# One block of gated attention and a mixture of experts on one core: the shared expert of a block runs behind the MLP of the next, weight splits move to VectorE, two normalizations share one chain, and q stays unnormalized

## The reference

```python
x = x + ln(attn(ln(x)))              # x: 2048 tokens x 256, ln: no weight, eps 1e-5
x = x + ln(moe(ln(x)))

def attn(x):                         # 16 heads of 16
    h = ln(x) * ln1w + ln1b
    xc = silu(causal_conv(h, 4 taps))
    q, k = l2norm(h @ Wq), l2norm(h @ Wk)          # per head, eps 1e-12
    v = ln_head(h @ Wv) * vnw + vnb
    u = sigmoid(xc @ Wig + big) * k * v
    mem = scan(m_t = gamma_t * m_(t-1) + u_t)      # gamma = sigmoid(xc @ Wg + bg)
    out = (ln_head(mem) * mnw + mnb) * q
    out = (ln_head(out) * gnw + gnb) * sigmoid(xc @ Wog + bog)
    h = x + out @ Wo
    return h + (silu(h2 @ Wgate) * (h2 @ Wval)) @ Wout     # h2 = ln(h)*ln2w+ln2b, width 1024

def moe(x):                          # 8 experts of width 176, the best 2; shared expert of width 704
    routed = sum of the 2 chosen experts, weighed by their softmax probabilities
    return routed + sigmoid(x @ shared_gate) * ((silu(x @ sg) * (x @ su)) @ sd)
```

## Time and profile before

| what | value |
|---|---|
| median of 3 runs | 705.24 us |
| the profiled execution: its own time | 704.88 us |
| its span, from the first to the last instruction | 703.1 us |
| PE busy | 557.0 us, 79% of the span |
| DVE busy | 417.2 us, 59% |
| ACT busy | 242.5 us, 34% |
| POOL busy | 128.3 us, 18% |
| chain that ended last | PE 50%, DVE 27%, issue 11%, POOL 6%, ACT 4% |

### The profile page before, as it was taken

The page is one execution under the profiler, slowest core; times in us unless marked ns, Lnnn a source line. Parts: engine busy times, 40 slices in busy tenths (PEclk is TensorE's granted clock), DMA queues, the critical chain, the costliest instruction groups (busy, mean ns, idle before and its releaser), DMA issues.

```text
span 703.1 us, 7640 instructions
## 1 busy us (share of the span) xinstructions
PE 557.0 (79%) x2332; PEld 417.0 (59%) x2332; DVE 417.2 (59%) x1313; ACT 242.5 (34%) x418; POOL 128.3 (18%) x120
## 2 busy tenths in 40 slices
PE   1742247995998998669999949999558999999493
PEld 1322035783876767458767827878446777777382
DVE  6386775348797467977637774711435455555147
ACT  3421335312537461226552224331012144444213
POOL 1142600112022012000513000210000423333300
PEclk9975667999799999959999976999858999999888
DMA  8940000000101000110100000010070233333343
GB/s 290 401 113 30 0 2 0 1 0 31 60 16 46 31 0 1 40 51 0 62 30 1 1 30 0 31 61 0 1 239 0 92 99 107 107 108 98 117 168 119
DMA packets 30570, 45.43 MB, mean 65 GB/s; under 512 B 3211, under 2 KB 25227, under 8 KB 30187
## 3 DMA queue, kind: packets, MB, share of 16 engines
q1 hardware_dynamic: 25539, 33.99, 14.9%
q0 software_dynamic: 3408, 9.38, 3.7%
q10 hardware_dynamic: 1584, 1.57, 0.7%
HBM read 28.60 MB, written 16.34 MB: 64 GB/s over the span
## 4 chain that ended last, share of the span: by engine, by line
PE 50%; DVE 27%; issue 11%; POOL 6%; ACT 4%; DMA 1%; POOLq 0%; DVEq 0%; ACTq 0%; SPq 0%
PE psum L682 11%; PE psum L647 8%; PE psum L648 7%; PE psum L649 7%; PE psum L707 6%; POOL y_routed L465 5%; PE psum L657 3%; DVE est L931 2%; PE psum L756 2%; DVE IG L1157 2%; PE psum L742 2%; PE psum L728 1%; DVE rt L912 1%; DVE rt L911 1%; PE psum L882 1%
## 5 line engine op out<-in xcount | busy, mean ns | idle before, releaser
L1215 DVE TENSOR_TENSOR SM<-SM,psum 128x512 f32<-128x512 f32 (+1 forms) x56 | 38.1, 683 | 85.5 <-ACT SM L576 85.3
L576 ACT ACTIVATE SM<-psum 128x512 f32<-128x512 f32 (+1 forms) x56 | 33.1, 595 | 147.2 <-PE psum L649 117.9
L456 POOL DMA_INDIRECT x_dispatched<-XN,dest x32 | 33.1, 1033 | 260.3 <-DVE XN L1278 251.8
L682 PE MATMUL psum<-WOU,SM 128*128 128x256 f32 x256 | 59.8, 379 | 0.0
L707 PE MATMUL psum<-WQKV,HT 128*128 128x512 f32 (+1 forms) x128 | 50.7, 544 | 8.1 <-ACT GA L563 3.3
L682 PEld LDWEIGHTS psum<-WOU,SM 128*128 128x128 f32 x256 | 48.2, 189 | 8.4 <-DVE SM L1215 0.5
L833 PE MATMUL psum<-RUP,GX 128*128 x156 | 52.7, 460 | 0.4 <-DVE GX L1293 0.4
L465 POOL DMA_INDIRECT y_routed<-GO,g_dest x39 | 37.9, 971 | 69.0 <-ACT GO L624 68.4
L682 PE MATMUL psum<-SDN,SM 128*128 128x256 f32 (+1 forms) x192 | 45.0, 381 | 0.7 <-DVE SM L1215 0.7
L647 PE MATMUL psum<-XTH,supH 128*128 128x512 f32 (+1 forms) x96 | 44.2, 460 | 0.8 <-issue 0.8
L707 PEld LDWEIGHTS psum<-WQKV,HT 128*128 128x128 f32 x128 | 26.3, 211 | 30.4 <-issue 24.3
(11 more groups left out here) (257 smaller groups left out, 1223.0 us busy)
## 6 DMA issues: line engine op xcount, KB each, us to landing
XG<-x_dispatched SPq DMA_DIRECT2D x39, 130.0 KB
YF<-y_routed SPq DMA_DIRECT2D x4, 1024.0 KB, 9.1
RUP<-rup SPq DMA_DIRECT2D x1, 2816.0 KB
X<-x SPq DMA_DIRECT2D x4, 512.0 KB, 6.8
x_after_attention<-X SPq DMA_DIRECT2D x4, 512.0 KB, 3.4
XF<-x_after_attention SPq DMA_DIRECT2D x1, 2048.0 KB, 8.1
out<-XF SPq DMA_DIRECT2D x4, 512.0 KB, 2.9
QKV<-x ACTq DMA_DIRECT2D x3, 512.0 KB, 3.6
```

The source lines that it names most:

```text
L456: nc.gpsimd.indirect_dma_start(XD[:, :], bass.IndirectOffsetOnAxis(dest[:, i, old + j:old + j + 1], 0), XN[:, j, :], None).then_inc(dispat ...
L682: last = nc.tensor.matmul(p_down[:, j // 2, (j % 2) * D:(j % 2 + 1) * D], SM[0:rows, g % 3, j * P:(j + 1) * P], weight[0:rows, m, :], star ...
L1215: nc.vector.tensor_tensor(SM[0:rows, g % 3, 0:tb], SM[0:rows, g % 3, 0:tb], p_pair(n)[1][0:rows, 0:tb], ALU.mult).then_inc(hid_ready, 1)
```

## The change

1. **The order.** The list of steps is now one list `ORDER` for all blocks. The shared expert of block b-1 stands behind `x2` of block b, ahead of `xt` of block b; `choose` and `rank` of b-1 stand among the MLP products of block b. In block 0 nothing stands behind `x2`. The shared expert of the last block comes last, as before. Since two steps now mix blocks, the counters (`HIDX`, `SLOT`, `done`) come from the list. `PLACE` has new numbers for it.
2. **Weight splits.** The `lo` halves are computed on DVE: two of the three weights after the first two tiles of `q` in block 0, the third (`sup`) among block 0's MLP products. In block 0, PE writes the four tiles of `q` into four different pairs of banks and no longer waits for ACT's copies.
3. **LayerNorms.** `ln0` computes both reciprocal roots in one chain of 8 values per token row. With v the variance, the root of the second LayerNorm is taken from (1 + eps) * v + eps * eps.
4. **q.** q is not divided by its norm. GpSimd multiplies each tile of q by the weight and by the bias of the norm as soon as ACT has squared it (three multiplications for a tile, with that of v; before: one, and three large ones later). The norm enters as the eps of the last LayerNorm per head, `qeps`, and `rs` treats 128 values instead of 192.
5. **Last pass.** `FIN` is two groups of 8 tiles.

```diff
+def _order():
+    def shared(b, at_rank):
+        out = []
+        for i in range(SMN + 3):
+            out += [("hid", b, i)] if i < SMN else []
+            out += [("sdn", b, i - 3)] if i >= 3 else []
+            out += [("rank", b, 0), ("choose", b, 3)] if i == 2 and at_rank else []
+        return out + [("shout", b, 0)]
+    order = []
+    for b in range(NB):
+        late = {0: [("choose", b - 1, 1)], 1: [("choose", b - 1, 2)], 2: [("rank", b - 1, 0), ("choose", b - 1, 3)]} if b > 0 else {}
+        for m in range(FM):
+            order += [("mup", b, m)] + ([("mdn", b, m - 1)] if m > 0 else []) + late.get(m, [])
+            order += [("split", 0, 2)] if (b, m) == (0, 4) else []
+        order += [("mdn", b, FM - 1), ("sum", b, 0), ("sum", b, 1), ("x2", b, 0), ("x2", b, 1)]
+        if b > 0:
+            order += shared(b - 1, False)
+        order += [("xt", b, 0), ("route", b, 0), ("choose", b, 0)]
...
-        [0, 2, 3, 4, 8, 13, 16, 16, 16, 16, 16, 17, 20, 21, 21, 21, 25, 25, 25, 26, 27, 27, 28, 30, 30, 33, 33,
+        [0, 0, 2, 2, 2, 2, 2, 2, 3, 3, 3, 3, 3, 4, 4, 4, 5, 6, 8, 8, 8, 8, 11, 11, 11, 11, 12,
...
-FIN = (4, 4, 4, 4)
+FIN = (8, 8)
...
# GpSimd, step q (scan on GpSimd is gone)
-                    nc.gpsimd.tensor_tensor(vj, vj, hvec[:, 0, :].unsqueeze(1).broadcast_to([P, HEADS, HD]),
-                                            ALU.mult).then_inc(v_scaled, 1)
-                        link(nc.gpsimd.tensor_tensor(q, q, per_head(rr[:, 0:nj, 0:HEADS]), ALU.mult))
-                        nc.gpsimd.tensor_tensor(k, q, per_dim(nj, 2), ALU.mult).then_inc(g_ready, 1)
-                        nc.gpsimd.tensor_tensor(w, q, per_dim(nj, 3), ALU.mult).then_inc(g_ready, 1)
+                    link(nc.gpsimd.tensor_tensor(heads(QB[:, m:m + 1, :]), qj, per_dim(1, 3), ALU.mult))
+                    nc.gpsimd.tensor_tensor(qj, qj, per_dim(1, 2), ALU.mult).then_inc(q_scaled, 1)
+                    nc.gpsimd.tensor_tensor(vj, vj, per_dim(1, 0), ALU.mult).then_inc(v_scaled, 1)
...
# VectorE
+                if stage == "split" and b == 0:
+                    k, _ = resident[m]
+                    dve.wait_ge(w_hi, m + 1)
+                    for c in range(C):
+                        nc.vector.tensor_tensor(lo[k][:, c, :], raw[k][:, c, :], f32(hi[k][:, c, :]), ALU.subtract).then_inc(w_lo, 1)
...
+                        step(rsqrt(r01[:, b % 2, :, 0:nj], *own))
...
+                        step(nc.vector.scalar_tensor_tensor(va[:, 0:G], va[:, 0:G], 1.0 / HD, qeps[:, 0:G], ALU.mult, ALU.add))
...
                 if stage == "wo":
+                    if b > 0:
+                        dve.wait_ge(x2_ready, b)
                     nc.vector.tensor_tensor(flat(HR[:, 0:nj, :]), flat(p_main)[:, 0:nj * D], flat(HN[:, 0:nj, :]), ALU.add).then_inc(hr_ready, 1)
...
# TensorE
                 if stage == "xt":
+                    if b > 0:
+                        pe.wait_ge(sh_ready, old)
```

More of the change, by code:

```diff
@@ L56 @@
 ATTENTION = (
-    [("q", j) for j in range(J)] + [("rs", 0), ("rs", 1), ("g", 0), ("g", 1)]
-    + [("u", i) for i in range(4)] + [("ut", 0), ("scan", 0), ("scan", 1), ("mt", 0), ("split", 0)]
-    + [("var", 0), ("rstd", 0), ("norm", 0), ("fetch", 0), ("g", 2), ("affine", 0), ("affine", 1), ("split", 1), ("split", 2)]
+    [("q", 0), ("split", 0), ("q", 1), ("split", 1)] + [("q", j) for j in range(2, J)] + [("rs", 0), ("rs", 1), ("g", 0), ("g", 1)]
+    + [("u", i) for i in range(4)] + [("ut", 0), ("scan", 0), ("scan", 1), ("mt", 0)]
+    + [("var", 0), ("rstd", 0), ("norm", 0), ("fetch", 0), ("g", 2), ("affine", 0), ("affine", 1)]
     + [("mean", 1), ("centre", 1), ("ln0", 0), ("var", 1), ("rstd", 1), ("norm", 1), ("og", 0), ("y0", 0), ("ln0", 1)]
@@ L63 @@
 AHEAD = [("ln0", i) for i in range(3)] + [("fetch", 0), ("ht", 0), ("xs", 0)] + [("conv", k) for k in range(KC)]
[L66 to L75, removed]
+def _order():
[16 more added lines that the diff above has]
+        order += [("xt", b, 0), ("route", b, 0), ("choose", b, 0)]
+    last = shared(NB - 1, True)
+    return order + last[:1] + [("choose", NB - 1, 1)] + last[1:3] + [("choose", NB - 1, 2)] + last[3:]
+ORDER = _order()
+HIDX = {step: g for g, step in enumerate(s for s in ORDER if s[0] in ("mup", "hid"))}
+SLOT = {step: n for n, step in enumerate(s for s in ORDER if s[0] in ("mup", "hid", "rank"))}
 PLACE = {
@@ L124, in steps @@
                  for i, s in enumerate(ATTENTION) if 0 <= b + (s in AHEAD) < NB]
-    experts = [(name, b, m) for b in range(NB) for name, m in EXPERTS[TILES[b]]]
-    for n, step in enumerate(experts):
+    for n, step in enumerate(ORDER):
         while attention and attention[0][0] <= n:
@@ L187, in build @@
         hst, hmv = sb("hst", [P, J, 6]), sb("hmv", [P, J, 2])
-        hva, hrs, hrt = (sb(k, [P, J]) for k in ("hva", "hrs", "hrt"))
+        hva, hrs, hrt = (sb(k, [P, 2, J]) for k in ("hva", "hrs", "hrt"))
         vec = sb("vec", [P, C, NVEC])
@@ L292, in v, with done @@
             return vec[:, c, i:i + 1]
-        def slot(b, h):
-            return SLOTS * b + h + (h >= FM + RANK_AT)
-        def rank_slot(b):
-            return SLOTS * b + FM + RANK_AT
         resident = [("wgt", 16), ("wvl", 16), ("sup", 16)]
-        W_UP, W_SHARED = 2, 3
+        W_UP, W_SHARED = 2 * C, 3 * C
         def hidden(stage, b, m):
-            h, rows = (m, P) if stage == "mup" else (FM + m, SM_ROWS[m])
-            return HIDDEN * b + h, slot(b, h), rows
+            step = (stage, b, m)
+            return HIDX[step], SLOT[step], P if stage == "mup" else SM_ROWS[m]
+        def done(stage, b, m):
+            return HIDX[(stage, b, m)] + 1
         block = ctx.enter_context(nc.Block())
@@ L361, in _ @@
                     load_x(b + 2)
-                if b + 1 < NB:
-                    sp.wait_ge(sh_ready, START[b + 1])
-                    sp.dma_start(tiles(SS, b), SH[:, 0:TILES[b], :]).then_inc(sh_kept, 16)
-            sp.wait_ge(up_psum, HIDDEN * (NB - 1) + FM)
+                if b > 0:
+                    sp.wait_ge(sh_ready, START[b])
+                    sp.dma_start(tiles(SS, b - 1), SH[:, 0:TILES[b - 1], :]).then_inc(sh_kept, 16)
+            sp.wait_ge(up_psum, done("mup", NB - 1, FM - 1))
             sp.wait_ge(x2_kept, 16 * NB)
@@ L430, in at @@
                     pool.wait_ge(sq_ready, old + m + 1)
[L431 to L450 removed]
+                    if b > 0 and m == 0:
+                        pool.wait_ge(wo_psum, b)
+                    qj, vj = heads(QKV[:, m:m + 1, 0:D]), heads(QKV[:, m:m + 1, 2 * D:3 * D])
+                    link(nc.gpsimd.tensor_tensor(heads(QB[:, m:m + 1, :]), qj, per_dim(1, 3), ALU.mult))
+                    nc.gpsimd.tensor_tensor(qj, qj, per_dim(1, 2), ALU.mult).then_inc(q_scaled, 1)
+                    nc.gpsimd.tensor_tensor(vj, vj, per_dim(1, 0), ALU.mult).then_inc(v_scaled, 1)
+                if (stage, m) == ("choose", 3):
                     pool.wait_ge(xn_ready, new)
@@ L519, in at @@
                         act.wait_ge(ss_done, n - 1)
+                    if b > 0 and m < 2:
+                        act.wait_ge(h2_lo, C * b)
                     nc.scalar.activation(SQ[n % 2], QKV[:, m, :], ACT.Square).then_inc(sq_ready, 1)
@@ L567, in at @@
                     if b > 0:
-                        act.wait_ge(up_psum, HIDDEN * (b - 1) + FM)
+                        act.wait_ge(up_psum, done("mup", b - 1, FM - 1))
                     for c in range(C):
@@ L587, in at @@
                     act.wait_ge(xt_psum, b + 1)
+                    if b > 0:
+                        act.wait_ge(up_psum, done("hid", b - 1, SMN - 1))
                     for c in range(C):
@@ L595, in at @@
                 if stage == "shout":
-                    act.wait_ge(hid_used, HIDDEN * (b + 1))
+                    act.wait_ge(hid_used, done("hid", b, SMN - 1))
                     act.wait_ge(shared_gate, b + 1)
@@ L706, in at @@
                         for c in range(C):
-                            last = nc.tensor.matmul(p_main[:, part, 0:cols.stop - cols.start], HT[:, c, tok], WQKV[:, c, cols],
+                            last = nc.tensor.matmul(q_banks(b, m)[:, part, 0:cols.stop - cols.start], HT[:, c, tok], WQKV[:, c, cols],
                                                     start=c == 0, stop=c == C - 1)
@@ L795, in at @@
                 if stage == "rank":
-                    n = rank_slot(b)
+                    n = SLOT[("rank", b, 0)]
                     pair_free(n)
@@ L908, in newton @@
             def newton(a, y, t, out):
+                if len(out.shape) > len(a.shape):
+                    a, y, t = (ap.rearrange("p (j h) -> p j h", h=out.shape[2]) for ap in (a, y, t))
                 settle()
@@ L1115, in at @@
                     dve.wait_ge(sq_ready, n + 1)
-                    if b > 0 and m == 0:
-                        dve.wait_ge(g_ready, 2 * b)
                     nc.vector.tensor_reduce(rr[:, m, :], by_head(SQ[n % 2]), AX_X,
@@ L1260, in at @@
```

(4 more changed lines are left out.)

145 lines of the change are left out of this document (72 added, 73 removed), and 56 rows, old and new, of the table PLACE.

## The result

The changed kernel takes 680.56 us (median of 4 runs, 680.3 to 681.84), the kernel before 705.12 us: a ratio of 0.965 with a 95% interval of 0.9636 to 0.9663. 674 us was forecast, with 648 to 696 as the range. The profiled execution is the one of 681.84 us, span 679.9 us against 703.1: 23.2 us less.

| part | before | after | difference | forecast |
|---|---|---|---|---|
| start to `q` of block 1 | 111.25 | 92.58 | -18.7 | -20.6 |
| `q` of block 1 to the end of the last shared expert | 449.6 | 437.1 | -12.5 | -17.7 |
| from there to the end, before the first sum | 107.7 | 110.1 | +2.4 | +2.8 |
| first sum of the last pass to the end | 34.6 | 40.1 | +5.6 | +4.3 |

A forecast was written before the change was run, and what follows sets the result against it. PE was taken to set the middle stretch, attention 0 being a chain through all engines. Span 703.1 - 20.6 (attention 0) - 17.7 (middle) + 7.1 (last pass) = 671.9, plus 1.8 outside = 673.7; forecast 674 us, range 648 to 696.

The forecast's parts named there:

- The stall of the first steps of `rs`: Attention 0: POOL ends about 1.3 us behind the last reduction and stalls these steps, a cost of 1.3 us.
- The two `rstd` chains: Attention 0: instructions that end as POOL's subtractions do no longer stall, saving 4.2 us and 5.8 us.
- `centre`: Attention 0: the copy of `sup` and the one ahead of it move from before ACT's square, saving 4.1 us.
- HR: Block 0's MLP beside attention 1: DVE runs `sum` ahead of the sum behind `wo`, leaving PE idle 6.3 us.
- the scan's wait: Block 2's MLP: attention 3's scan stands behind `sum` and `x2` on DVE, leaving PE idle 3.5 us.
- the hole: Behind block 3's MLP: PE waits while DVE does `sum` and `x2` before the first `hid` multiplication, 7.8 us idle.
- the wait for `low`: Last stage, at `rank`: PE's wait of 2.8 us goes, since `choose` starts a step earlier.
- the hole costs twice: Middle stretch: PE's clock is low behind the hole before `xt`; low-clock price 32 us before, 23.5 after.
- The waits did not hide themselves: Rival, chance 0.2: PE's queue absorbs the waits; middle stretch 405 us, total 647 us.
- That attention 1 is exposed further: Rival, chance 0.13: attention 1's chain is 10 us longer and the clock stays low; middle stretch 454, total 695 us.
- The slower one: Rival, chance 0.05: DVE's queue lets PE fall dry 13.3 us in each of blocks 1 to 3; 704 to 710 us.
- That the order brings nothing: Rival, chance 0.07: the order alone brings nothing, the rest does; middle stretch 450 +/- 5, total 691 us.

The follow-up runs named there:

- the run with the splits in holes: Changed kernel with last pass in four groups of four, two shared steps ahead of x2's statistics (last block), two weight splits moved where VectorE idles: 663.8 us.

## Why the prediction was right, and where its sizes were off

All three parts came out worse than forecast, by 1.9, 5.2 and 0.9 us, so none of them hid an error of another; inside the middle stretch errors of both signs did meet.

**Attention 0** gave 18.7 of 20.6 us. `ln0`: its last instruction starts at 8.89 in place of 11.70, 2.8 of 3.0. `q`: `rs` starts at 31.73 in place of 35.70 us, 4.0, and less the 2.8 of `ln0` that is 1.2 of 2.0; the run with the splits in holes shows the cause, DVE's splits and ACT's casts between the tiles. I had them lie beside ACT's copies. The stall of the first steps of `rs` was to cost 1.3; `rs` took 4.8 us in place of 4.6, since its narrower chain gives most of it back. `u` starts as one instruction of 1.23 us, 1.8 as forecast. The scan takes 2.46 for 3.61, 1.15 of 1.0. The two `rstd` chains run without a stall, 4.2 and 5.8 us as forecast. `centre` was the wrong one: 2.7 us in place of 4.1. ACT's square is done at 64.7, but DVE's queue has the statistics of `ln0` of block 1 ahead of what reads it, and these wait for the load of x:

```profile
64.04 1.40 DVE L944 BATCH_NORM_STATS2 hst<-QKV 128x6 f32<-128x256 f32 x4 [1.00 <-DMA QKV<-x]
```

The three together are 12.8 us where the sum has 14.1, and the splits alone gave 12.6 to the time. The last us is the clock: `wo` in attention 0 takes 6.33 us in place of 5.35, at a mean granted clock of 0.58 in place of 0.69.

**The middle stretch** gave 12.5 of 17.7 us; of the 5 us that are missing, -2.1 are an error in idle time and +7.2 one in busy time.
- The idle time, 46.4 of 48.5, hides errors of both signs. Blocks 0 to 2 came to 28.7 in place of 36.5. HR (5.8 of 6.3) and the wait before `wo` (3.8 of 3.9) were right and XN had no wait, but the scan's wait was 2.3 instead of 3.5, and the sum behind `wo` of block 1's MLP (2.6) did not wait at all. The last stage came to 17.7 in place of 12: the hole is 10.5 instead of 7.8, as I walked DVE's queue and not ACT's, and the wait for `low` stayed at 2.8 where I said that it goes.
- The term that was mis-sized is the clock, "the hole costs twice". I took 32 us of the busy time as its price before and 23.5 after, 8.5 less, and the work at full clock as the same 360 us. PE's busy time fell by 1.6 us (392.3 to 390.7) where the sum has 8.8. Cut into stretches of 0.5 us, with each stretch's busy time weighed by its granted clock, the two traces give 28.3 us of price before and 24.6 after: 3.7 less. Of the 43 us of granted time missing before, 15 and not 11 stand where PE is idle, and of 32 after, 7; there they cost nothing. The work at full clock comes out by the same reckoning as 364.0 us before and 366.1 after; the cause of these 2 us stays open.
- Why the price fell so little: behind the last `xt` before, with its hole of 13.3 us, 11.9 us of busy time are at 1.2 GHz; after, with no hole there, they are still 9.4, and 3.8 more stand behind the hole where it is now. Cutting that one from 10.5 to 3.3 us left PE's busy time as it was, and with the old order it was 2.1 us more. Before, the hole stood right ahead of `xt`, so that the earlier trace rows could not tell the two apart. That the short products and waits of `xt` and `route` lower the clock is read from the rows above; no run changed them alone.

**The last pass** cost 8.0 of 7.1 us: the wait for YF 2.4 of 2.8, the rest 5.6 of 4.3. Up to the end of the additions that rest is 3.8 us, near the 3.5 of the sum (statistics of 2.75 + 0.64 us, and 16 additions at the end instead of 8); the last store took 1.8 us more (4.7 against 2.9), not 0.8. This is the part that I called a loss, and it is.

**Rivals.** The waits did not hide themselves (the middle stretch took 437.1 us, not 405). That attention 1 is exposed further did not come (17.3 idle in its stage, 19 forecast). The slower one needed a middle stretch over 463 us; it also sets its price against 23 us of idle time in blocks 1 to 3, where the walk has 8 + 9.5 + 12 = 29.5. That the order brings nothing was refuted by the run with the old order. What the profile was to show held in all but two points: the hole (10.5, not 7 to 8), and the stretch from first sum to end, 40.1 us, at the edge of 38 to 40.

## What to carry to other kernels

A wait that one engine's queue makes is found by walking every queue that the data crosses: here, by the timeline, ACT's order made 2.6 us of a hole that seemed to be DVE's, and moving two steps ahead of it was worth 7.3 us. A bulk copy or subtraction belongs where its engine is idle, and not on GpSimd beside a chain of small VectorE instructions; that one edit was worth 12.6 us. Wait time that an edit fills was worth little more than its own length here: count a gain in clock only where the rows show that the slow stretch stands behind that wait and not behind the short products next to it.
